# Long cross-attention of a Perceiver block: head pairs joined at their border, and a wait for GpSimd moved to where the keys are made

## The chip, the cores and the metric

The kernel runs on one core of a Trainium2 chip. The metric is the device time of one execution in microseconds. A core has TensorE (PE in the rows; PEld is its weight load), VectorE (DVE), ScalarE (ACT), GpSimd (POOL) and a queue for transfers (SP). Each engine works through its own list in order and waits for the others on semaphores.

## The reference, cut to what matters

Two layers are computed on 256 query tokens; the change touches one attention of the second layer only. With `x` of 256 x 512, a context of 4096 x 128 and 16 heads:

```python
q_hk  = (hidden_q @ Wq.T).reshape(B, S, 16, 128)
q_big = rope(einsum('bshk,hkq->bshq', q_hk, w_kc_q))      # 384 wide
kv_r  = rope(kv_c)                                        # 4096 x 128
q_r   = einsum('bshq,hqr->bhsr', q_big, W_qr)             # 64 wide
k_r   = einsum('bld,hdr->bhlr', kv_r, W_kr)
attn  = softmax(einsum('bhsr,bhlr->bhsl', q_r, k_r))      # 256 x 4096 per head
ctx_c = einsum('bhsl,bld->bhsd', attn, kv_r)
out   = einsum('bhsd,hkd->bhsk', ctx_c, w_kc_kv) @ Wo.T
```

## The kernel before, in words

Products that need more precision than one pass gives are split: a value is rounded to a high part (`keyH`, `pH`, `kvH`, `qsH`, `wkrH`, made on ScalarE) and what is left is the low part (`keyL`, `pL`, made on VectorE; `kvL`, `wkrL`, `qsL`, made on GpSimd). A product is then high by high, high by low and low by high.

**Projections.** TensorE's loop `for n in range(XH)` goes over the 16 heads: `p1(n + 1)` (8 matmuls), `p2(n)` (6 matmuls), and `p3` for a finished pair (12 matmuls). ScalarE copies the result of `p1` to `qh`, which `p2` needs and which frees bank 6 for the next `p1`. VectorE rotates the result of `p2` (`rotated(n)`: four products of PSUM with a table, the four small ones into `qm2` together with the large one into `qb`, and then the sum `qb + qm2`, L1064, both in SBUF). `p2(n + 1)` waits for the products of `rotated(n)`. Into this loop the keys of the first head pair are set at the projections that `KEYS_AT` names (`keys(0, c)`, eight stretches c of 512 keys; ScalarE makes `keyH`, VectorE `keyL`), and their scores at projections 6 to 13. The keys overwrite the rotated context in SBUF (`kvr`), from which GpSimd makes `kvL` in a single instruction; so ScalarE waits for `kvL_ready`, ahead of its first `qh`. After the loop come `keys(1, 0)`, six dummy matmuls (`stay_awake`, which only keep TensorE busy) and `p3(7)`.

**Pairs.** Then a loop over the 8 head pairs p, each over 8 stretches c of 512 keys, each over four halves e; i = 4c + e counts the 32 halves of a pair. For each half TensorE turns the exponentials (`turn(p, i)`, four transposes), ScalarE evicts them as `pH`, VectorE as `pL`, and two halves later TensorE multiplies them with the context (`weigh(p, i)`, six matmuls into bank 6, which collects the whole pair). Meanwhile the next pair is prepared: at e = 1 its keys c + 1 (`next_keys`, always through bank 7), evicted by ScalarE (`high_keys`) at e = 1 and by VectorE (`low_keys`) at e = 2; after the four halves its scores c (`scores`), which VectorE takes out in four tiles with a running maximum during the next stretch (`scores_out`, one in each half, ahead of `pL`). The four tiles of the last stretch come after the last `pL`, each followed by the small reduction that gives the row maximum (`nmX`). ScalarE makes the first stretch of exponentials from it (`first_exps`, four tiles), and the others one for each half. The finished bank 6 is copied out by `contexts_out` after the first half of the next pair, and goes through `values` and `head_out` (bank 7 too) in stretches 1 to 5. Before those, TensorE waits for the low keys in bank 7:

```python
if p and 1 <= c <= 5 and more:
    pe.wait_ge(keyL_ready, (p + 1) * NCH + c + 2)
```

At the end of a pair TensorE finishes `weigh` of its last halves before it turns anything of the next.

Of the kernel before, what the change touches and what calls it, by code (L numbers as in the profile page):

```python
# [8 lines left out]
T = 256  # L9
# [13 lines left out]
XH, XK, XQ, XR = 16, 128, 384, 64  # L23
# [3 lines left out]
NCH = L // CH  # L27
# [13 lines left out]
XP = XH // 2  # L41
SLOTS = 2 * NCH
HALVES = 4 * NCH
KEYS_AT = {1: (0,), 2: (1, 2), 3: (3, 4), 4: (5, 6), 5: (7,)}
SCORES_AT = {6 + c: c for c in range(NCH)}
TILES = ((0, 0), (1, 0), (0, 1), (1, 1))
TILES_LAST = ((0, 0), (0, 1), (1, 0), (1, 1))
# [5 lines left out]
F32 = mybir.dt.float32  # L53
# [32 lines left out]
def perceiver(nc, a, out):  # L86
    ctx = ExitStack()
    with ctx:
# [541 lines left out]
        def _(act):  # L630
# [128 lines left out]
            def high_keys(p, c, bank=7):  # L759
                act.wait_ge(key_ps, p * NCH + c + 1)  # L760
                wait(act, sX_ps, 2 * ((p - 1) * NCH + c + 1))
                act.activation(keyH[:, c * CH:(c + 1) * CH], PS[:, bank, :], ACT.Copy).then_inc(keyH_ready, 1)
# [4 lines left out]

            high_parts(0)
            high_parts(1)
            act.wait_ge(kvL_ready, 1)  # L770
            for n in range(XH):
                act.wait_ge(p1_done, n + 1)
                wait(act, p2_done, n - 1)
                act.activation(qh[:, n % 2], PS[:, 6, 0:T], ACT.Copy).then_inc(qh_ready, 1)
                for c in KEYS_AT.get(n - 1, ()):
                    high_keys(0, c, 0 if c % 2 else 7)
                if n % 2 == 0 and n >= 4:
                    ranks_out((n - 4) // 2)
                    if (n - 4) // 2 < 2:
                        high_query((n - 4) // 2)  # L780
# [7 lines left out]

            def first_exps(p):
                wait(act, csum_done, p - 1)  # L790
                for h, q in TILES_LAST:
                    exps(p, h, q, 0)

            def contexts_out(p):
# [10 lines left out]
            for p in range(XP):  # L805
                for c in range(NCH):
                    for e in range(4):
                        i = 4 * c + e
                        act.wait_ge(t_done, HALVES * p + i + 1)
                        wait(act, v_done, HALVES * p + i - 3)  # L810
                        act.activation(pH[:, i % 4], PS[:, 2 + i % 2, :].rearrange("p (k t) -> p k t", t=T), ACT.Copy).then_inc(pH_ready, 1)  # L811
                        if i == 0 and p:
                            contexts_out(p - 1)
                        if i == 8 and p:
                            values_out(p - 1)
                        if c + 1 < NCH:
                            exps(p, e // 2, e % 2, c + 1)
                        if e == 1 and c + 1 < NCH and p + 1 < XP:
                            high_keys(p + 1, c + 1)
                        if e == 1 and c + 1 == NCH and p + 2 < XP:  # L820
                            high_keys(p + 2, 0)
                        if i == 14 and p + 2 < XP:
                            high_parts(p + 2)
                            high_query(p + 2)
                if p + 1 < XP:
                    first_exps(p + 1)
# [73 lines left out]
        def _(dve):  # L900
# [165 lines left out]
            def low_keys(p, c, bank=7):  # L1066
                dve.wait_ge(keyH_ready, p * NCH + c + 1)
                at = slice(c * CH, (c + 1) * CH)
                dve.tensor_tensor(keyL[:, at], PS[:, bank, :], keyH[:, at].bitcast(F32), ALU.subtract).then_inc(keyL_ready, 1)  # L1069

            def scores_out(p, c, e):

                h, q = (TILES_LAST if c == NCH - 1 else TILES)[e]
                dve.wait_ge(sX_ps, 2 * (p * NCH + c) + q + 1)
                dve.tensor_scalar(sp_[:, h, q, c * CH:(c + 1) * CH], PS[:, 4 * q + h, :], 1.0, None, ALU.mult, ALU.max,  # L1075
                                  accum_out=cmax[:, h, q, c:c + 1]).then_inc(sX_out, 1)
                if c == NCH - 1:
                    dve.wait_ge(sX_out, 4 * (p * NCH + c) + e + 1)
                    dve.tensor_reduce(nmX[:, p % 2, h, q:q + 1], cmax[:, h, q], AX.X, ALU.max, negate=True).then_inc(nm_ready, 1)  # L1079
# [34 lines left out]
            for p in range(XP):  # L1114
                for c in range(NCH):
                    for e in range(4):
                        i = 4 * c + e
                        if c and p + 1 < XP:
                            scores_out(p + 1, c - 1, e)
                        if e == 0 and p and c in (3, 4, 5, 6):  # L1120
                            add_out(p - 1, (c - 3) // 2, (c - 3) % 2, 7)
                        dve.wait_ge(pH_ready, HALVES * p + i + 1)
                        dve.tensor_tensor(pL[:, i % 4], PS[:, 2 + i % 2, :].rearrange("p (k t) -> p k t", t=T), pH[:, i % 4].bitcast(F32),  # L1123
                                          ALU.subtract).then_inc(pL_ready, 1)
                        if e == 2 and c + 1 < NCH and p + 1 < XP:
                            low_keys(p + 1, c + 1)
                        if e == 2 and c + 1 == NCH and p + 2 < XP:
                            low_keys(p + 2, 0)
                        if c == 1 and e % 2:
                            row_max(2 * p, e // 2)  # L1130
                        if c == 6 and e % 2 and p + 1 < XP:
                            row_max(2 * p + 1, e // 2)
                if p + 1 < XP:
                    for e in range(4):
                        scores_out(p + 1, NCH - 1, e)
                dve.wait_ge(exp_done, 2 * SLOTS * (p + 1))
                dve.tensor_reduce(recX[:, p % 2], csum[:, p % 2], AX.X, ALU.add).then_inc(csum_done, 1)
                dve.wait_ge(csum_done, p + 1)
                dve.reciprocal(recX[:, p % 2], recX[:, p % 2]).then_inc(recX_ready, 1)
# [122 lines left out]
        def _(pe):  # L1262
# [208 lines left out]
            def p1(n, i, b):  # L1471

                pe.wait_ge(wqX_in[b], (i + 1) * 16)
                wait(pe, qh_ready, n)
                wait(pe, qr_ready, (n - 3) // 2)
                for kt in range(KT):
                    mm = pe.matmul(PS[:, 6, 0:T], wqX[:, b, kt, :], xnT[:, kt, :], start=(kt == 0), stop=(kt == KT - 1))
                mm.then_inc(p1_done, 1)
# [82 lines left out]
            for n in range(XH):  # L1561
                if n + 1 < XH:
                    p1(n + 1, (n + 1) // 2, (n + 1) % 2)
                p2(n, n // 2, n % 2)
                if n % 2 and n >= 3:
                    p3((n - 3) // 2)
                for c in KEYS_AT.get(n, ()):
                    wait(pe, keyL_ready, c - 1)
                    keys(0, c, 0 if c % 2 else 7)
                if n in SCORES_AT:  # L1570
                    pe.wait_ge(keyL_ready, NCH)
                    scores(0, SCORES_AT[n])
# [9 lines left out]
            for p in range(XP):  # L1582
                more = p + 1 < XP
                for c in range(NCH):
                    last = more and c + 1 == NCH
                    for e in range(4):
                        i = 4 * c + e
                        turn(p, i)
                        if i >= 2 and not (last and e == 3):
                            weigh(p, i - 2)  # L1590
                        if e == 1 and p and c:
                            pe.wait_ge(vX_ready, p - (c == 1))
                            wait(pe, oX_added, 4 * (p - 1) + min(max(c - 2, 0), 4))
                        if e == 1 and c + 1 < NCH and more:
                            next_keys(p + 1, c + 1)
                        if e == 1 and c + 1 == NCH and p + 2 < XP:
                            next_keys(p + 2, 0)
                    if p and 1 <= c <= 5 and more:
                        pe.wait_ge(keyL_ready, (p + 1) * NCH + c + 2)
                    if p and c == 1:  # L1600
                        values(p - 1)
                    if p and 2 <= c <= 5:
                        pe.wait_ge(vX_ready, p)
                        head_out(p - 1, (c - 2) // 2, c % 2, 7)
                    if more:
                        scores(p + 1, c)
                if more:
                    weigh(p, HALVES - 3)
                for i in (HALVES - 2, HALVES - 1):
                    weigh(p, i)  # L1610
            values(XP - 1)
            pe.wait_ge(vX_ready, XP)
# [217 lines left out]
```

## Time and profile before

| | |
|---|---|
| median of 3 runs | 1105.48 us (1104.18 to 1107.18) |
| the profiled execution's own time | 1111.0 us |
| its span | 1109.3 us |
| TensorE busy | 1029.9 us (93%) |
| VectorE busy | 730.3 us (66%) |
| ScalarE busy | 573.2 us (52%) |
| GpSimd busy | 268.1 us (24%) |
| projections of this attention | about 345 to 450 us of the span |
| pair 0 | about 450 to 509 us |
| pairs 1 to 6 | 66 us each, about 509 to 905 us |
| pair 7 | about 905 to 955 us |

Times in the rows are microseconds from the start of the span. In a timeline row the first number is the start, the second the duration of the (merged) instructions, and what stands in brackets is how long the engine had sat idle before them and what ended that. Matmuls overlap in the pipeline, so the start-to-start distance of two rows says more than their durations.

### The profile page before, as it was taken

The numbers are of one execution on the slowest core, as the hardware profiler recorded it, in microseconds if no ns is written. First come the engines' busy times: TensorE is split into PE (matmuls) and PEld (weight loads), VectorE is DVE, ScalarE is ACT, GpSimd is POOL, SyncE is SP. The second block draws the span as 40 slices with busy tenths as digits, with TensorE's granted clock in tenths as the row PEclk, the third lists the DMA queues.
The fourth block names the chain that finished last, engine by engine and source line by source line (L and its number), as shares of the span: only waits on it lengthen the run. The fifth ranks groups of instructions, "written<-read, shape, count | busy, mean of one in ns | idle before, by whom it ended". The sixth has DMA issues, their size and how long they took to land.

```text
span 1109.3 us, 18581 instructions
## 1 busy us (share of the span) xinstructions
PE 1029.9 (93%) x6815; PEld 813.9 (73%) x6829; DVE 730.3 (66%) x1441; ACT 573.2 (52%) x1227; POOL 268.1 (24%) x209
## 2 busy tenths in 40 slices
PE   7989999999995998999999999999999999898996
PEld 5545889999993765787777877777777779676743
DVE  3656455655533899678787777778778786463634
ACT  3345345444423210677667676675776668343423
POOL 6810144434433000022220212222021111103412
PEclk9999899999998999999999999999999999999998
DMA  9450176666502332111120111202021124403010
GB/s 275 103 230 1 23 239 210 229 232 220 200 13 90 103 89 76 47 29 32 29 55 2 53 32 30 56 1 59 27 60 40 40 64 87 165 37 157 0 62 19
DMA packets 72253, 97.49 MB, mean 88 GB/s; under 512 B 35665, under 2 KB 53233, under 8 KB 71026
## 3 DMA queue, kind: packets, MB, share of 16 engines
q1 hardware_dynamic: 72178, 96.49, 28.3%
q8 instruction: 47, 0.77, 0.3%
q14 instruction: 28, 0.23, 0.1%
HBM read 91.58 MB, written 4.90 MB: 87 GB/s over the span
## 4 chain that ended last, share of the span: by engine, by line
PE 65%; DVE 18%; ACT 9%; issue 4%; POOL 2%; DMA 1%; SPq 0%; ACTq 0%; DVEq 0%; POOLq 0%
PE PS L1418 12%; PE PS L1545 8%; PE PS L1522 7%; PE PS L1534 6%; PE PS L1437 5%; DVE pL L1123 4%; DVE scores L1075 4%; ACT pH L811 3%; PE PS L1559 3%; ACT scores L787 3%; PE PS L1507 3%; DVE keyL L1069 2%; PE PS L1266 2%; PE PS L1629 2%; PE PS L1712 1%
## 5 line engine op out<-in xcount | busy, mean ns | idle before, releaser
L1123 DVE TENSOR_TENSOR pL<-PS,pH 128x512 fp32r<-128x512 f32 x256 | 176.4, 689 | 85.9 <-ACT pH L811 84.9
L811 ACT ACTIVATE pH<-PS 128x512 fp32r<-128x512 f32 x256 | 152.6, 596 | 121.7 <-PE PS L1534 121.7
L787 ACT ACTIVATE scores<-scores,nmX 128x512 f32<-128x512 f32 x256 | 185.4, 724 | 15.8 <-DVE nmX L1079 15.8
L1075 DVE TENSOR_SCALAR_CACHE_REDUCE scores<-PS 128x512 f32<-128x512 f32 x256 | 173.0, 682 | 21.8 <-PE PS L1522 21.8
L1534 PE MATMUL PS<-ident,scores 128*128 128x128 f32 x1024 | 156.6, 277 | 10.0 <-DVE pL L1123 9.9
L1545 PE MATMUL PS<-pH,kvH 128*128 128x256 f32 x512 | 164.6, 321 | 0.0
L1534 PEld LDWEIGHTS PS<-ident,scores 128*128 128x128 f32 x1024 | 117.2, 141 | 41.9 <-DVE pL L1123 21.4
L1545 PE MATMUL PS<-pL,kvH 128*128 128x256 f32 x512 | 144.4, 282 | 0.0
L1545 PE MATMUL PS<-pH,kvL 128*128 128x256 f32 x512 | 143.9, 281 | 0.0
L1545 PEld LDWEIGHTS PS<-pH,kvH 128*128 128x128 f32 x512 | 97.2, 190 | 2.7 <-DVE pL L1123 2.7
L1545 PEld LDWEIGHTS PS<-pL,kvH 128*128 128x128 f32 x512 | 97.7, 191 | 0.0
L1545 PEld LDWEIGHTS PS<-pH,kvL 128*128 128x128 f32 x512 | 96.9, 189 | 0.0
L982 DVE TENSOR_TENSOR gL<-rawG,gH 128x1536 fp32r<-128x1536 f32 x16 | 56.9, 3557 | 29.7 <-ACT gH L671 29.5
L545 POOL TENSOR_TENSOR dL<-rawD,dH 128x1536 fp32r<-128x1536 f32 x16 | 56.4, 3525 | 49.8 <-ACT dH L715 49.8
L566 POOL TENSOR_TENSOR wkrL<-wkr,wkrH 128x128 fp32r<-128x128 f32 x8 | 3.6, 456 | 251.4 <-ACT wkrH L752 251.4
L1522 PE MATMUL PS<-keyH,qsH 64*128 64x512 f32 x256 | 59.6, 461 | 4.6 <-DVE scores L1075 4.1
L1418 PE MATMUL PS<-xH,gH 128*128 128x256 f32 x192 | 55.9, 291 | 2.4 <-DVE uL L982 2.4
L1418 PE MATMUL PS<-xH,gL 128*128 128x256 f32 x192 | 55.5, 289 | 0.0
L1418 PE MATMUL PS<-xL,gH 128*128 128x256 f32 x192 | 55.5, 289 | 0.0
L1418 PE MATMUL PS<-xH,uH 128*128 128x256 f32 x192 | 55.0, 286 | 0.0
L1418 PE MATMUL PS<-xL,uH 128*128 128x256 f32 x192 | 54.9, 286 | 0.0
L1418 PE MATMUL PS<-xH,uL 128*128 128x256 f32 x192 | 54.9, 286 | 0.0
(309 smaller groups left out, 2243.4 us busy)
## 6 DMA issues: line engine op xcount, KB each, us to landing
rawG<-in_wg SPq DMA_DIRECT2D x16, 768.0 KB, 5.6
rawU<-in_wu SPq DMA_DIRECT2D x16, 768.0 KB, 7.1
rawD<-in_wd SPq DMA_DIRECT2D x16, 768.0 KB, 6.3
xn<-in_w SPq DMA_DIRECT2D x11, 512.0 KB, 3.9
wblk<-blocks SPq DMA_DIRECT2D x4, 1056.0 KB, 9.5
wb<-w_rows SPq DMA_DIRECT2D x32, 128.0 KB, 3.3
wqX<-in_wqX SPq DMA_DIRECT2D x16, 256.0 KB, 2.6
woX<-in_woX SPq DMA_DIRECT2D x8, 512.0 KB, 4.1
```

What stands on the lines that cost most here:

```text
L545: pool.tensor_tensor(dL[:, b].rearrange("p m n -> p (m n)"), rawD[:, b], dH[:, b].rearrange("p m n -> p (m n)").bitcast(F32), ALU.subtract ...
L787: act.activation(at, at, ACT.Exp, bias=nmX[:, p % 2, h, q:q + 1], accum_out=csum[:, p % 2, NT * h + q, c:c + 1]).then_inc(exp_done, 1)
L811: act.activation(pH[:, i % 4], PS[:, 2 + i % 2, :].rearrange("p (k t) -> p k t", t=T), ACT.Copy).then_inc(pH_ready, 1)
L982: dve.tensor_tensor(lo[b][:].rearrange("p k m n -> p (k m n)"), raw[:, b], hi[b][:].rearrange("p k m n -> p (k m n)").bitcast(F32), ALU.su ...
L1075: dve.tensor_scalar(sp_[:, h, q, c * CH:(c + 1) * CH], PS[:, 4 * q + h, :], 1.0, None, ALU.mult, ALU.max, accum_out=cmax[:, h, q, c:c + 1] ...
L1123: dve.tensor_tensor(pL[:, i % 4], PS[:, 2 + i % 2, :].rearrange("p (k t) -> p k t", t=T), pH[:, i % 4].bitcast(F32), ALU.subtract).then_in ...
L1418: mm = pe.matmul(PS[:, 3 * b + m, j * T:(j + 1) * T], w[b][:, kt, m, :], v[:, kt, :], start=(kt == 0 and c == 0), stop=(kt == KT - 1 and c ...
L1437: mm = pe.matmul(PS[:, 6 + t, :], h[:, b, m, t * P:(t + 1) * P], w[:, b, m, :], start=(first and m == 0 and c == 0), stop=(last and m == 2 ...
L1507: mm = pe.matmul(PS[:, bank, :], w[:, p % 2, :], v[:, c * CH:(c + 1) * CH], start=(j == 0), stop=(j == 2))
L1522: mm = pe.matmul(PS[:, 4 * q + h, :], w[rank, p % 2, q * P:(q + 1) * P], v[rank, c * CH:(c + 1) * CH], start=(j == 0), stop=(j == 2), skip ...
L1534: mm = pe.transpose(PS[:, 2 + i % 2, m * T + q * P:m * T + (q + 1) * P], sp_[:, h, q, tile * P:(tile + 1) * P], ident[:])
L1545: mm = pe.matmul(PS[:, 6, h * T:(h + 1) * T], w[:, 4 * c + 2 * u + m, :], v[:, i % 4, m, :], start=(i == 0 and m == 0 and k == 0), stop=(c ...
```

## The change

- `KEYS_AT`: the first pair's keys are made at projections 2 to 5, two at each, where they were at 1 to 5 (1, 2, 2, 2, 1).
- ScalarE's wait for `kvL_ready` moves from before the first `qh` to before the first `keyH`.
- `low_keys` stands ahead of `pL` in its half, where it stood behind it.
- Two of the four last score tiles of the next pair are taken out before the pair's last `pL`, two behind it.
- `first_exps` makes three tiles; the fourth is made behind the next pair's first `pH`. `contexts_out` moves from behind the first `pH` to behind the second.
- TensorE's order at the border: `weigh` of halves 28 and 29 comes after the last scores, and `weigh` of halves 30 and 31 after the next pair's `turn` 0 and 1.
- Ten dummy matmuls stand ahead of `p2(14)` and ten ahead of `p2(15)`.

```diff
-KEYS_AT = {1: (0,), 2: (1, 2), 3: (3, 4), 4: (5, 6), 5: (7,)}
+KEYS_AT = {2: (0, 1), 3: (2, 3), 4: (4, 5), 5: (6, 7)}
...
             high_parts(1)
-            act.wait_ge(kvL_ready, 1)
             for n in range(XH):
...
                 for c in KEYS_AT.get(n - 1, ()):
+                    if c == 0:
+                        act.wait_ge(kvL_ready, 1)
                     high_keys(0, c, 0 if c % 2 else 7)
...
-                for h, q in TILES_LAST:
+                for h, q in TILES_LAST[0:3]:
                     exps(p, h, q, 0)
...
-                        if i == 0 and p:
+                        if i == 0:
+                            exps(p, 1, 1, 0)
+                        if i == 1 and p:
                             contexts_out(p - 1)
...
-                        dve.wait_ge(pH_ready, HALVES * p + i + 1)
-                        dve.tensor_tensor(pL[:, i % 4], PS[:, 2 + i % 2, :].rearrange("p (k t) -> p k t", t=T), pH[:, i % 4].bitcast(F32),
-                                          ALU.subtract).then_inc(pL_ready, 1)
                         if e == 2 and c + 1 < NCH and p + 1 < XP:
                             low_keys(p + 1, c + 1)
                         if e == 2 and c + 1 == NCH and p + 2 < XP:
                             low_keys(p + 2, 0)
+                        if i == HALVES - 1 and p + 1 < XP:
+                            for tile in range(2):
+                                scores_out(p + 1, NCH - 1, tile)
+                        dve.wait_ge(pH_ready, HALVES * p + i + 1)
+                        dve.tensor_tensor(pL[:, i % 4], PS[:, 2 + i % 2, :].rearrange("p (k t) -> p k t", t=T), pH[:, i % 4].bitcast(F32),
+                                          ALU.subtract).then_inc(pL_ready, 1)
...
                 if p + 1 < XP:
-                    for e in range(4):
-                        scores_out(p + 1, NCH - 1, e)
+                    for tile in range(2, 4):
+                        scores_out(p + 1, NCH - 1, tile)
...
+                if n >= XH - 2:
+                    stay_awake(10, 7)
                 p2(n, n // 2, n % 2)
...
-                        if i >= 2 and not (last and e == 3):
+                        if i >= 2 and not (last and e >= 2):
                             weigh(p, i - 2)
+                        if i < 2 and p:
+                            weigh(p - 1, HALVES - 2 + i)
...
-                if more:
-                    weigh(p, HALVES - 3)
-                for i in (HALVES - 2, HALVES - 1):
+                for i in (HALVES - 4, HALVES - 3) if more else (HALVES - 2, HALVES - 1):
                     weigh(p, i)
```

## Rows read from the trace of the kernel before

**Rows 1.** Windows: stretch, length, busy PE, PEld, DVE, ACT, POOL, granted clock, DMA, GB/s

```profile
509.00:575.00 66.00, 62.71 (x454) 51.15 (x452) 51.86 (x123) 45.49 (x108) 12.41 (x9) 1.00 0.15 36
...
443.40:449.00 5.60, 5.52 (x18) 3.09 (x18) 3.45 (x7) 0.00 (x0) 0.00 (x0) 0.50 0.00 0
...
913.00:917.00 4.00, 3.83 (x20) 3.83 (x21) 1.64 (x4) 3.24 (x10) 0.00 (x0) 0.57 0.00 0
```

**Rows 2.** Waits, 509 to 905 us: total us, times, longest

```profile
PE PS L1559 <- DVE keyL L1069: 6.9, 24, 0.5
```

**Rows 3.** Timeline at the start of the projections

```profile
345.22 1.97 PE L1477 MATMUL PS<-xnT,wqX 128*128 128x256 f32 x8 [1.78 <-issue]
...
356.49 0.38 ACT L774 ACTIVATE qh<-PS 128x256 f32<-128x256 f32 x1 [8.52 <-POOL kvL L562]
...
357.02 3.68 PE L1477 MATMUL PS<-xnT,wqX 128*128 128x256 f32 x8 [9.84 <-ACT qh L774]
...
366.31 0.96 DVE L1058 TENSOR_TENSOR qb<-PS,cosQ 128x768 f32<-128x768 f32 x1 [0.72 <-PE PS L1486]
...
371.22 1.29 ACT L762 ACTIVATE keyH<-PS 128x512 fp32r<-128x512 f32 x2 [2.10 <-PE PS L1507]
```

**Rows 4.** Timeline of VectorE and GpSimd in an earlier stage

```profile
167.78 3.81 DVE L982 TENSOR_TENSOR gL<-rawG,gH 128x1536 fp32r<-128x1536 f32 x1 [1.79 <-ACT gH L671]
171.51 1.75 DVE L982 TENSOR_TENSOR uL<-rawU,uH 128x1536 fp32r<-128x1536 f32 x1
...
166.45 3.52 POOL L545 TENSOR_TENSOR dL<-rawD,dH 128x1536 fp32r<-128x1536 f32 x1 [2.41 <-ACT dH L715]
```

**Rows 5.** Timeline inside pair 2: ends of stretches 4 and 6

```profile
615.97 0.69 DVE L1123 TENSOR_TENSOR pL<-PS,pH 128x512 fp32r<-128x512 f32 x1 [0.54 <-ACT pH L811]
616.58 0.68 DVE L1069 TENSOR_TENSOR keyL<-PS,keyH 128x512 fp32r<-128x512 f32 x1
...
616.82 0.27 PE L1545 MATMUL PS<-pH,kvL 128*128 128x256 f32 x1
617.31 1.13 PE L1559 MATMUL PS<-woX,xnT 128*128 128x512 f32 x2 [0.22 <-DVE keyL L1069]
...
633.55 0.27 PE L1545 MATMUL PS<-pH,kvL 128*128 128x256 f32 x1
633.76 0.50 PE L1522 MATMUL PS<-keyH,qsH 64*128 64x512 f32 x2
```

**Rows 6.** Timeline at the border from pair 1 to pair 2

```profile
575.03 0.68 DVE L1075 TENSOR_SCALAR_CACHE_REDUCE scores<-PS 128x512 f32<-128x512 f32 x1
...
575.78 0.50 PE L1522 MATMUL PS<-keyH,qsH 64*128 64x512 f32 x2 [0.62 <-DVE scores L1075]
...
578.77 0.72 ACT L787 ACTIVATE scores<-scores,nmX 128x512 f32<-128x512 f32 x1
...
580.77 0.59 ACT L796 ACTIVATE xnT<-PS 128x512 f32<-128x512 f32 x1
...
581.65 0.66 PE L1534 MATMUL PS<-ident,scores 128*128 128x128 f32 x4 [1.00 <-DVE pL L1123]
...
583.33 0.66 PE L1534 MATMUL PS<-ident,scores 128*128 128x128 f32 x4 [0.31 <-DVE pL L1123]
```

**Rows 7.** Timeline at the end of the projections

```profile
437.49 1.46 PE L1486 MATMUL PS<-qh,kcq 128*128 128x256 f32 x6
...
440.85 0.96 DVE L1058 TENSOR_TENSOR qb<-PS,cosQ 128x768 f32<-128x768 f32 x1
...
443.48 2.90 PE L1486 MATMUL PS<-qh,kcq 128*128 128x256 f32 x6 [4.53 <-DVE qm L1062]
446.31 2.83 PE L1498 MATMUL PS<-qb,xn 128*64 128x256 f32 x12
...
450.17 1.24 PE L1266 MATMUL PS<-busyB,identE 128*128 128x512 bf16 x5
451.35 1.52 PE L1498 MATMUL PS<-qb,xn 128*64 128x256 f32 x12
```

## The prediction

> **What bounds the kernel now.** I read the page first: TensorE is busy for 93% of the span, so only stretches in which it waits, or runs at half its clock, can give time back. The windows give a table by stage. In a pair of the middle it is busy for 62.71 of 66.00 us at full clock, VectorE for 51.86, ScalarE for 45.49 [rows 1]: TensorE sets the pace there, and the change can touch at most 3.3 us of a pair. Then the waits of pairs 1 to 6: TensorE waits 24 times, 6.9 us in all, for `keyL` ahead of `head_out` [rows 2]. Last the timeline at the edited places. It shows four of them: the start of the projections (ScalarE idle for 8.52 us and TensorE for 9.84 us, for GpSimd's `kvL`) [rows 3], their end (4.53 us idle, then half clock) [rows 1, 7], the low keys in each stretch [rows 5], and the border of two pairs [rows 6].
>
> **Wait for GpSimd moved to the keys.** ScalarE was free at 356.49 - 8.52 = 347.97; the first `p1` ended at 345.22 + 1.97 = 347.19 [rows 3]. So `qh(0)` starts at 348.0, and the second `p1` at 348.5 where it was at 357.02: 8.5 us. After 9.84 us of idleness TensorE ran that `p1` in 3.68 us; the one before it, after 1.78 us of idleness, took 1.97 [rows 3]. With only some 1.3 us idle now I take 1.97, 1.7 us more. By TensorE alone the gain is 10.2 to 10.3.
>
> VectorE takes a part of it back. Its first sum `qb + qm2` (L1064) ended 0.72 before 366.31, at 365.6, so it began at 364.6; 10.3 earlier is 354.3. But GpSimd's `kvL` runs until ScalarE is released by it, at 356.45 [rows 3]. In an earlier stage such a pair of instructions met: VectorE's 1536-element subtraction from two SBUF tensors started at 167.78 while GpSimd was in one that ended at 169.97; it took 3.81 us, its twin just after 1.75, and it ended 1.6 us after GpSimd did [rows 4]. So I count the sum as beginning when `kvL` ends: done at about 357.3. The next rotation begins then, against 366.31 before [rows 3]: from here on everything is 9.0 us early instead of 10.3.
>
> The Trainium skill, "SBUF — State Buffer", section "SBUF: two separate sides", speaks against this edit too: a VectorE instruction with two SBUF inputs and a GpSimd instruction that reads SBUF exclude each other for the whole of whichever began first. By that rule, the rows agree, the gain is 9.0; without it, 10.3.
>
> The moved wait itself should cost nothing: `keyH` of projection 2 starts at 371.22 before, about 362 now, 5.5 us after `kvL` [rows 3]. `wkrL` is queued behind `kvL` on GpSimd and wanted about a microsecond earlier than `keyH`; also there in time. The transfers of `wqX` and `kcq` move with `p1` and `p2`; the two buffers of each were loaded long before.
>
> **Keys at 2 to 5.** Projection 1 loses a set of keys, 5 gains one. The step from projection 1 to 2 is set by VectorE's rotation, so nothing is won there; in 5 the second key is ahead of `qr`, for which the next `p1` waits. Two evictions take 1.29 us [rows 3], so one more costs 0.65 to 0.7. Loss 0.7. Start in all: 9.0 - 0.7 = 8.3 (bounds 6 and 9.6).
>
> **Dummy matmuls at 14 and 15.** Five take 1.24 us [rows 7], about 0.22 each, so ten take 2.2. Those ahead of `p2(14)` push it back by 2.2 us; but its result, there at 437.49 + 1.46 = 438.95, is read by VectorE only at 440.85 [rows 7], when the scores are out. 1.9 us hide most of it; 0.35 is lost. Those ahead of `p2(15)` lie in the 4.53 us in which TensorE waits for VectorE, and keep it busy. The window behind that wait has a granted clock of 0.50, that is 1.2 GHz [rows 1]: `p2(15)` takes 2.90 us, and `p3(6)`, 12 matmuls, 2.83; the same 12 at full clock take 1.52 [rows 7]. I take 1.46 for `p2(15)`, as `p2(14)` took [rows 7]. It then starts at 443.48 + 0.35 = 443.83 and ends at 445.3, and `p3(6)` ends at 446.75 instead of 449.14: 2.4 us. `keys(1, 0)`, the six dummies and `p3(7)` follow, at 448.95 instead of 451.35 [rows 7]. ScalarE's exponentials hang on `p3(6)` and start 2.4 earlier too; one of four of them now stands behind `pH(0)`, which helps pair 0 a little. Sum 2.5 (bounds 1.5 and 3.1).
>
> **Low keys ahead of `pL`.** In stretch 4, `head_out` starts 0.49 us after the last matmul of `weigh`; where nothing is waited for, the distance is 0.21 [rows 5]. That is 0.28 lost, of which 0.22 counts as idle. Over the 24 waits the mean idle is 0.29 [rows 2], so 0.36 lost; the fifth wait of a pair, at `values`, I take at 0.26. Per pair 4 x 0.36 + 0.26 = 1.7. Can it all come back? `keyL` is issued 0.61 after `pL`, and VectorE idles 0.54 ahead of that `pL`, for `pH` [rows 5]; `keyH` is ScalarE's instruction before that `pH`. So `keyL` ends 0.6 to 1.1 us earlier, more than the longest wait of 0.5 counted (0.59 in true distance). `pL` slips by 0.1 to 0.2 us, but the first to need it is a `turn` after the scores, over 2 us later. Pairs 1 to 6: 6 x 1.7 = 10.1 (bounds 5 and 10.5; in pair 0 the wait does not exist).
>
> **The border.** Before, TensorE loses there about 0.9 us at the scores' second half (575.78), 1.2 at 581.65 and 0.5 at 583.33 [rows 6]. I lay the new order from VectorE's fourth tile of scores (575.03). It comes 0.5 earlier, since `keyL` fills an idle wait. The second half of the last scores follows 0.75 later as before. The third exponential was at 575.03 + 3.74 = 578.77 [rows 6]; the same instructions lie between in the new order, but VectorE's second tile now stands ahead of `pL` and waits some 0.37 for TensorE. So 574.53 + 3.74 + 0.37 = 578.65: 0.1 gained. From there ScalarE is busy without a pause. The copy of the contexts began 2.00 us after the third exponential [rows 6]; now one exponential (0.7) and one `pH` (0.5) more stand ahead of it, so it begins at 581.85 and ends at 582.45. `weigh(0)` of the new pair waits for it: 582.5, where it was at 582.06. `turn(3)` follows 0.8 later, 583.3, against 583.33 before. TensorE's early wait is gone and comes back as a wait for the contexts. I take 0 for each of the 7 borders (bounds 0.6 lost, by a `turn` held up behind the copy, and 1.9 gained, the idle that rows 6 count: 0.62 + 1.00 + 0.31). Into pair 7 the clock fell to a mean of 0.57 for 4 us [rows 1]; whether it does again I leave at 0.
>
> **Sum.** 8.3 + 2.5 + 10.1 + 0 = 20.9. The span would be 1088.4 and the profiled execution's own time 1111.0 - 20.9 = 1090.1. That execution stands 5.5 above the median of the runs; taken off the median, 1105.5 - 20.9 = **1084.6 us**.
>
> **The rivals.**
> - *The joined border pays.* ScalarE's start is what counts, and if the two early tiles let it run without a gap, about 1 us of the 1.9 comes back per border: 7 us more, 1077.6. For it: the order plainly separates the two engines' work. Against: the copy before `weigh(0)`. Chance 0.15.
> - *The late copy costs.* If `contexts_out` slips a further half microsecond, each border loses 0.5 to 1: about 5 us, 1089.6. For it: no slack in my layout. Chance 0.17.
> - *Head of the line at `keyL`.* VectorE now waits for `keyH` with `pL` and a tile of scores behind it. If `keyH` is late in half the stretches, 5 of the 10.1 go: 1089.7. Against: `keyH` stands ahead of `pH` on ScalarE. Chance 0.09.
> - *No change.* The gains of the start are a shift that nothing after it takes back, so this needs both other terms to turn. Chance 0.03.
> - *Slower.* The clock falls at every border: the new order has short waits at three places, and the one border with little other work already fell to 0.57 [rows 1]. A microsecond at 1.2 GHz loses half of one. The 20.9 are gone when each of 7 borders loses 3 us, that is 6 us at half clock each; with 8 us each, 1084.6 + 28 = 1112.6. Against: the windows of a pair show 1.00. Chance 0.03.
>
> **How the numbers follow.** The forecast has the rest, 0.53. A tenth of a per cent is about a microsecond here; differences under 0.3%, 3.3 us, can't be told from no change. The first four cases, 0.94, are faster by more than that; same 0.03; slower 0.03. The range 1077 to 1092 takes the two dearer rivals whole, half of the cheaper one, and the forecast with its own bounds.
>
> **What would show it.** Right: `qh(0)` near 348, the sum L1064 ending just after `kvL` with a duration of about 3 us, `keyH` with no wait for GpSimd; clock 1.00 where rows 1 show 0.50; no wait `head_out` for `keyL`; pairs of 64.4 us; at the border a wait of `weigh` for ScalarE's copy of the contexts. Wrong: pairs under 64 us (the border pays) or over 65; a granted clock under 1 at borders; a wait for the loads of `wqX` at the start.

## The result and the profile after

| | before | after |
|---|---|---|
| median (4 runs each, same chip) | 1105.39 us | 1079.51 us (1077.56 to 1080.04) |
| ratio | | 0.9761, 95% interval [0.9743, 0.9779] |
| the profiled execution: own time, span | 1111.0, 1109.3 us | 1079.65, 1077.9 us |

The change gains 25.9 us by the medians, 26.4 by the ratio (24.4 to 28.4 by the interval). The gains of the versions below are worked out from the ratio. The forecast was 1084.6 us with a range of 1077 to 1092; it was 5 us too careful. The page of the changed kernel; the columns are busy us, share of the span, instructions:

```profile
PE 1020.7 (95%) x6849; PEld 809.4 (75%) x6849; DVE 734.0 (68%) x1441; ACT 572.2 (53%) x1227; POOL 269.1 (25%) x209
```

TensorE was busy for 9.2 us more before, though the change adds 20 dummy matmuls (4.6 us): what went are, as far as the rows below show, matmuls at half its clock (`p2(15)` in 2.90 us and now in 1.53) and a longer duration right after a wait (`head_out` in 1.13 us and now in 1.02). The rest of the gain is idle time. Windows of the changed kernel, columns as in [rows 1]: a stretch of the pairs, the end of the projections, the border into pair 7, and two stretches at the first keys:

```profile
509.00:575.00 66.00, 64.22 (x475) 53.44 (x475) 54.05 (x127) 47.89 (x115) 12.47 (x8) 1.00 0.15 36
...
432.00:442.00 10.00, 9.48 (x54) 5.02 (x52) 7.31 (x15) 3.57 (x7) 0.00 (x0) 1.00 0.01 2
...
879.00:885.00 6.00, 4.59 (x37) 3.94 (x36) 3.71 (x11) 5.42 (x14) 0.00 (x0) 1.00 0.55 152
...
352.00:359.00 7.00, 3.99 (x18) 3.26 (x19) 6.79 (x9) 0.40 (x2) 3.76 (x3) 1.00 0.36 103
359.00:363.00 4.00, 4.00 (x12) 3.18 (x11) 3.21 (x7) 1.19 (x2) 0.00 (x0) 0.58 0.17 49
```

The reader sees TensorE busy for 64.22 of 66 us where it was 62.71, and 1.00 at the two places where [rows 1] has 0.50 and 0.57. But a new low clock, 0.58, stands at the first keys.

The waits of the changed kernel from 495 to 880 us (total us, times, longest). No line of TensorE names `keyL` any more, where [rows 2] had 24 waits. At the border the wait of `weigh` for the copy `xnT` is new, and the one for a tile of scores, 3.8 us in 6 waits before (509 to 905 us), has grown:

```profile
DVE keyL L1072 <- ACT keyH L762: 5.9, 6, 1.0
PE PS L1551 <- ACT xnT L797: 5.5, 6, 0.9
PE PS L1528 <- DVE scores L1078: 5.4, 7, 0.9
```

The start of the projections (timeline of the changed kernel), to be held against [rows 3]:

```profile
345.87 8.84 POOL L562 TENSOR_TENSOR kvL<-kvr,kvH 128x4096 fp32r<-128x4096 f32 x1 [7.90 <-ACT kvH L747]
...
346.61 1.97 PE L1483 MATMUL PS<-xnT,wqX 128*128 128x256 f32 x8 [1.21 <-ACT qh L773]
...
352.51 3.02 DVE L1067 TENSOR_TENSOR qb<-qb,qm 128x768 f32<-128x768 f32 x1
...
358.27 1.54 PE L1492 MATMUL PS<-qh,kcq 128*128 128x256 f32 x6 [2.39 <-DVE qm L1065]
...
360.04 0.63 PE L1513 MATMUL PS<-kvTL,wkrH 128*128 128x512 f32 x1
```

The second `p1` starts while `kvL` has just begun, and takes 1.97 us. The sum `qb + qm2` meets `kvL` and lasts 3.02 us. TensorE then waits 2.39 us at `p2(2)`, its clock falls, and a key matmul takes 0.63 us where it takes 0.39 at full clock. The end of the projections:

```profile
432.54 2.32 PE L1272 MATMUL PS<-busyB,identE 128*128 128x512 bf16 x10
435.38 1.53 PE L1492 MATMUL PS<-qh,kcq 128*128 128x256 f32 x6 [0.52 <-DVE qm L1065]
436.84 1.52 PE L1504 MATMUL PS<-qb,xn 128*64 128x256 f32 x12
...
440.10 0.72 ACT L788 ACTIVATE scores<-scores,nmX 128x512 f32<-128x512 f32 x1
```

`p2(15)` and `p3(6)` take 1.53 and 1.52 us where [rows 7] have 2.90 and 2.83. The end of stretch 4 in pair 2, which answers to [rows 5]:

```profile
600.56 0.28 PE L1551 MATMUL PS<-pH,kvL 128*128 128x256 f32 x1
600.67 1.02 PE L1565 MATMUL PS<-woX,xnT 128*128 128x512 f32 x2
```

The distance from the last `weigh` matmul to `head_out` is 0.11 us, where it was 0.49 with the wait, and the two matmuls of `head_out` take 1.02 instead of 1.13. And the border from pair 1 to 2, which answers to [rows 6]:

```profile
558.93 0.69 DVE L1072 TENSOR_TENSOR keyL<-PS,keyH 128x512 fp32r<-128x512 f32 x1
...
560.13 0.68 DVE L1078 TENSOR_SCALAR_CACHE_REDUCE scores<-PS 128x512 f32<-128x512 f32 x1
...
560.88 0.50 PE L1528 MATMUL PS<-keyH,qsH 64*128 64x512 f32 x2 [0.85 <-DVE scores L1078]
...
567.30 0.58 ACT L797 ACTIVATE xnT<-PS 128x512 f32<-128x512 f32 x1
...
568.03 0.36 PE L1551 MATMUL PS<-pH,kvH 128*128 128x256 f32 x1 [0.91 <-ACT xnT L797]
```

The wait for `pL` became one for the copy of the contexts (0.91), and the wait for a tile of scores grew from 0.62 to 0.85.

**Where the time went.** The gain of the profiled execution is 1109.3 - 1077.9 = 31.4 us. Of it 1.78 lie ahead of the edited code (`kvH` starts at 343.97 before, at 342.19 after) and 1.77 behind pair 7: the two executions differ there by chance, and these two explain most of why the spans differ by more than the medians. The clock shows it: both kernels run the same instructions there, and the mean granted clock is 0.72 from 118 to 130 us and from 965 to 977 before, against 0.86 from 117 to 129 and from 936 to 948 after. The rest I read from `kvH` to the first exponential, and then between the first matmuls of `scores` of each stretch, which every version has in the same order:

| part | before | after | gained |
|---|---|---|---|
| `kvH` to the first exponential (450.89 and 440.10) | 106.92 | 97.91 | 9.0 |
| from there to the first `scores` of pair 1 (518.55 and 506.85) | 67.66 | 66.75 | 0.9 |
| from there to the first `scores` of pair 6 (849.09 and 823.25), five pairs | 330.54 | 316.40 | 14.1 |
| the rest of pair 6 and pair 7, what is left of 31.4 - 3.55 | | | 3.8 |

The 9.0 are 6.6 at the start (read at `p2(6)`: 391.86 before and 383.44 after, less the 1.78) and 2.4 at the end of the projections. Of the 3.8, 2.9 lie before the last `scores` of pair 6 (904.50 and 875.79) and 0.9 behind them. In pair 1 the stretches, from one `scores` to the next, took 8.37, 8.65, 8.36, 8.37, 8.34, 7.04 and then 16.94 us for the last one with the border; now they take 7.90, 7.88, 7.89, 7.88, 7.88, 7.03 and 16.75. A pair went from 66.07 to 63.21 us.

### The profile page after: what moved, and what is told of

Same layout as the page of the kernel before. It is cut to its first block, busy times and chain, and to the rows that moved or that the text cites. A ratio compares the mean times of both kernels' runs of the same rounds, so it can differ in the third digit from the quotient of the medians.

```text
span 1077.9 us, 18635 instructions
## 1 busy us (share of the span) xinstructions
PE 1020.7 (95%) x6849; PEld 809.4 (75%) x6849; DVE 734.0 (68%) x1441; ACT 572.2 (53%) x1227; POOL 269.1 (25%) x209
## 4 chain that ended last, share of the span: by engine, by line
PE 79%; DVE 12%; ACT 5%; issue 2%; DMA 1%; POOL 1%; SPq 0%; DVEq 0%; ACTq 0%; POOLq 0%
PE PS L1551 16%; PE PS L1424 12%; PE PS L1540 10%; PE PS L1528 8%; PE PS L1443 5%; PE PS L1513 4%; DVE scores L1078 2%; PE PS L1565 2%; PE PS L1272 2%; PE PS L1637 2%; ACT scores L788 1%; PE PS L1720 1%; PE PS L1646 1%; PE PS L1324 1%; PE PS L1483 1%
## 5 line engine op out<-in xcount | busy, mean ns | idle before, releaser
L1528 PEld LDWEIGHTS PS<-keyH,qsH 64*128 64x128 f32 x256 | 24.0, 183 | 42.3 <-issue 24.5
```

Of the source, the lines that this page charges most:

```text
L1528: mm = pe.matmul(PS[:, 4 * q + h, :], w[rank, p % 2, q * P:(q + 1) * P], v[rank, c * CH:(c + 1) * CH], start=(j == 0), stop=(j == 2), skip ...
```

## The experiments

The first question was where the gain of the pairs comes from. Theory A: low keys ahead of `pL` are worth nearly 3 us per pair, and the joined border nothing. Theory B, by my own sizes: a removed wait is worth what I forecast (1.7 us per pair), and the joined border brings the rest. A kernel's time stands beside runs of the kernel before on the same chip.

**Low keys alone.** The kernel before with

```diff
+                        if e == 2 and c + 1 < NCH and p + 1 < XP:
+                            low_keys(p + 1, c + 1)
...
                         dve.wait_ge(pH_ready, HALVES * p + i + 1)
                         dve.tensor_tensor(pL[:, i % 4], ...
-                        if e == 2 and c + 1 < NCH and p + 1 < XP:
-                            low_keys(p + 1, c + 1)
```

> The kernel before with one part alone: low_keys ahead of pL. Theory A (the term was mis-sized): a wait of TensorE ahead of head_out costs 0.48 us and not 0.28, because the load of its weights is no longer hidden behind the last weigh, and pair 0 gains 0.2 us a stretch too, because VectorE's fourth tile of scores is out sooner. Then stretches 1 to 5 of pairs 1 to 6 give 2.7 us a pair and pair 0 about 1: 17 us, about 1088.5. Theory B (the term was right, the border gave the rest): 10 us, about 1095.5, and stretches 3 to 5 shorter by 0.28 each.

1088.23 us against 1107.38, ratio 0.9827 [0.9799, 0.9855]: 19.2 us. From the first `scores` of pair 1 to that of pair 2 are 62.84 us (515.44 to 578.28), 3.2 less than before, and below the 63.21 of the changed kernel; two later pairs of this execution were 0.9 and 0.6 us longer than such pairs are in the versions below. From the first exponential to the last `scores` of pair 6 this one edit gains 18.6 us, more than the whole change there (17.9). B falls. In pair 0, where there is no wait for `keyL`, the stretches fall from 7.20 to 7.03 us too: VectorE's tile of scores comes earlier, and TensorE's second half of `scores` follows the first after 0.80 us instead of 0.87, with its two matmuls at 0.39 instead of 0.50.

**The start alone** (`KEYS_AT` and the moved wait):

```diff
+KEYS_AT = {2: (0, 1), 3: (2, 3), 4: (4, 5), 5: (6, 7)}
...
-            act.wait_ge(kvL_ready, 1)
...
+                    if c == 0:
+                        act.wait_ge(kvL_ready, 1)
```

> The kernel before with the start alone: the wait for GpSimd at the first key, and the first pair's keys at projections 2 to 5. By the prediction's term 8.3 us, 1097. In the changed kernel's trace TensorE fell to half clock at the keys of projection 2, which took 1.6 us of it; Theory A: that happens here too, 6.5 us, 1099. Theory B (the low clock there was chance): 8.3 us.

1099.47 us, ratio 0.9935 [0.9912, 0.9959]: 7.2 us. From `kvH` to the first exponential are 100.36 us, 6.56 less than before. The low clock at the first keys is there too (and in two versions below with the same start, the one without the border part and the one with the copy of the contexts back: 0.67 and 0.66 from 356 to 361 us). Its windows:

```profile
352.00:359.00 7.00, 4.60 (x20) 3.65 (x18) 5.68 (x7) 0.38 (x1) 2.49 (x3) 0.90 0.30 87
359.00:363.00 4.00, 4.00 (x15) 3.25 (x15) 3.52 (x7) 1.20 (x2) 0.00 (x0) 0.76 0.18 49
```

**The dummies alone** (`stay_awake(10, 7)` ahead of `p2(14)` and `p2(15)`):

> The kernel before with the twenty dummy matmuls ahead of p2(14) and p2(15) alone. By the prediction's term 2.4 us at the first exponentials, 1103; granted clock 1.00 where it was 0.50. The rival: the dummies only keep TensorE from work that was ready, and the exponentials start no sooner, 1105.4.

1105.0 us, ratio 0.9986 [0.9964, 1.0009]: the median can't tell it from nothing, but the trace can. From `kvH` (342.96) to the first exponential (447.49) are 104.53 us, 2.39 less than before, with the clock at 1.00.

**The joined border alone** (the other three edits undone):

```diff
+                for h, q in TILES_LAST[0:3]:
...
+                        if i == 0:
+                            exps(p, 1, 1, 0)
+                        if i == 1 and p:
                             contexts_out(p - 1)
...
+                        if i < 2 and p:
+                            weigh(p - 1, HALVES - 2 + i)
```

> The kernel before with the border alone: three first exponentials, the contexts' copy behind the second pH, two score tiles ahead of the last pL, weigh of halves 30 and 31 behind the next pair's turns; low_keys stays behind pL. By the prediction's layout 0 per border. Here VectorE's fourth tile is not 0.5 us earlier, so the third exponential and all behind it come 0.4 later: 0 to 3 us slower in all, 1105 to 1108. Theory B (the border gave what the prediction lacked): 1 us less per border, 1098.

1108.18 us, ratio 1.001 [0.9989, 1.003]. A pair takes 66.40 us (515.86 to 582.26), 0.33 more than before. TensorE's waits from 510 to 910 us, which holds six borders (total us, times, longest):

```profile
PE PS L1527 <- DVE scores L1077: 6.8, 6, 1.3
PE PS L1550 <- ACT xnT L796: 5.5, 6, 0.9
```

They are 1.13 and 0.92 us per border, together more than the 0.62 + 1.00 + 0.31 of [rows 6]. From the second half of the last scores (573.09) to the third exponential (576.43) it takes 3.34 us, where [rows 6] have 2.99.

**The changed kernel without the border part.**

> The changed kernel without its border part (start, low_keys and dummies stay): four first exponentials, the contexts' copy behind the first pH, all four score tiles behind the last pL, weigh in the old order. If the border is worth nothing in its place (the prediction's layout: 0.1 us at each of 7), the time is that of the changed kernel, 1079.5 to 1080.5. If it gave what the prediction lacked, about 5 us more, 1085. The trace of the changed kernel shows TensorE idle for 0.85 and 0.91 us at a border; here waits of about 0.4, 1.0 and 0.3 as before.

1076.65 us against 1105.08, ratio 0.9732 [0.9697, 0.9767]: not slower, and in the trace 0.37 us per pair faster (62.84, from 504.75 to 567.59). Its border from pair 1 to 2:

```profile
558.01 0.68 DVE L1076 TENSOR_SCALAR_CACHE_REDUCE scores<-PS 128x512 f32<-128x512 f32 x1
...
558.75 0.50 PE L1523 MATMUL PS<-keyH,qsH 64*128 64x512 f32 x2
...
564.62 0.66 PE L1535 MATMUL PS<-ident,scores 128*128 128x128 f32 x4 [1.01 <-DVE pL L1128]
...
566.29 0.66 PE L1535 MATMUL PS<-ident,scores 128*128 128x128 f32 x4 [0.31 <-DVE pL L1128]
```

Its third exponential, and that of the changed kernel:

```profile
561.74 0.72 ACT L788 ACTIVATE scores<-scores,nmX 128x512 f32<-128x512 f32 x1
...
564.21 0.72 ACT L788 ACTIVATE scores<-scores,nmX 128x512 f32<-128x512 f32 x1 [0.58 <-DVE nmX L1082]
```

The 0.62 that [rows 6] show ahead of the second half of the scores is gone without the border part: `keyL` now fills an idle wait of VectorE, so its tile of scores is out in time. The joined order brings a wait back at that place, since it takes the `weigh` of one half (28; that of 29 stood behind the scores already) away from ahead of the scores, which had covered VectorE's tile. But this wait by itself costs nothing: counted from the first matmul of the scores before (551.17 here, 553.31 in the changed kernel), the second half of the last scores starts 7.58 us later here and 7.57 there, and the `weigh` that went is only done later. What does come later is ScalarE's work, since VectorE's second tile, now ahead of `pL`, waits for TensorE: the third exponential follows the second half of the scores after 2.99 us here (558.75 to 561.74), as before (575.78 to 578.77), and after 3.33 in the changed kernel (560.88 to 564.21). Idle per border: 1.32 us here, 0.85 + 0.91 = 1.76 in the changed kernel; the difference of 0.44 stands beside 0.37 of the period.

**The copy of the contexts back behind the first `pH`** (`if i == 0 and p: contexts_out(p - 1)`, after the fourth exponential):

> The changed kernel with contexts_out back behind the first pH (but behind the fourth exponential, which stands there now). The prediction says that the late copy gives back what the joined border wins, because weigh(0) waits for it. The copy then ends about 1.2 us earlier and weigh(0) with it, but turn(3) next waits for pL(1), which the copy now delays by 0: so 0.2 us at each border, 1.4 in all, 1078. If the copy is the only thing in the way, 0.9 at each border, 6 us, 1073.5. If the copy waits for weigh of half 31 on TensorE and holds ScalarE up with it: slower, 1082.

1077.26 us, ratio 0.9743 [0.9711, 0.9774]. A pair takes 63.09 us (504.34 to 567.43), 0.12 less than in the changed kernel. The late copy carries a third of the border's loss. The rest, 0.25, goes with the later third exponential: it still stands 3.34 us behind the second half of the scores (558.34 to 561.68), where it is 2.99 without the border part. The wait for a tile of scores, 5.4 us over 7 borders in either kernel's wait table, is the same in both and doesn't delay what stands behind it.

**`kvL` in four instructions of GpSimd.** The question is whether VectorE's sum is shut out for as long as one GpSimd instruction lasts, or is slowed by the traffic of both engines.

```diff
-            pool.tensor_tensor(kvL[:], kvr[:], kvH[:].bitcast(F32), ALU.subtract).then_inc(kvL_ready, 1)
+            for part in range(4):
+                rows = slice(8 * part, 8 * part + 8)
+                ins = pool.tensor_tensor(kvL[:, rows], kvr[:, rows], kvH[:, rows].bitcast(F32), ALU.subtract)
+            ins.then_inc(kvL_ready, 1)
```

> The changed kernel with GpSimd's kvL in four instructions of 1024 elements a partition instead of one of 4096. If VectorE's sum of two SBUF tensors is shut out for the whole of a GpSimd instruction, it now ends within 2.2 us of when it is ready instead of at the end of kvL: its duration falls from 3.0 us to at most 2.2, or below 1.9 where it comes right behind a boundary, and all that follows is 0.8 to 1.3 us earlier, if TensorE's clock does not eat it. If the two instructions merely share bandwidth, the duration stays near 3 us.

1076.33 us, ratio 0.973 [0.9699, 0.9761]. Its timeline (the four instructions merged, then the first and the fourth alone) and windows:

```profile
346.35 10.00 POOL L564 TENSOR_TENSOR kvL<-kvr,kvH 128x1024 fp32r<-128x1024 f32 x4 [8.93 <-ACT kvH L750]
...
346.35 2.35 POOL L564 TENSOR_TENSOR kvL<-kvr,kvH 128x1024 fp32r<-128x1024 f32 x1 [8.93 <-ACT kvH L750]
...
352.99 1.14 DVE L1070 TENSOR_TENSOR qb<-qb,qm 128x768 f32<-128x768 f32 x1
...
353.28 3.08 POOL L564 TENSOR_TENSOR kvL<-kvr,kvH 128x1024 fp32r<-128x1024 f32 x1
...
357.31 1.53 PE L1495 MATMUL PS<-qh,kcq 128*128 128x256 f32 x6 [0.95 <-DVE qm L1068]
```

```profile
352.00:359.00 7.00, 5.03 (x23) 4.11 (x23) 5.61 (x11) 0.77 (x2) 4.85 (x4) 1.00 0.40 118
359.00:363.00 4.00, 4.00 (x20) 3.32 (x18) 3.94 (x8) 1.58 (x3) 0.00 (x0) 1.00 0.24 52
```

The sum takes 1.14 us instead of 3.02 in the midst of GpSimd's work, so it is the length of one GpSimd instruction that counts. The exclusion shows on both sides: the first three instructions take 2.35 us each, and the third ends at 353.32; the sum ends 0.8 us after that, as it ended 0.8 us after the single long `kvL` (355.53 and 354.71); and the fourth, which meets the sum, takes 3.08, 0.73 more than the others. The sum came only 0.33 us before the third ended. Right behind the start of one it would have stood there for up to 2.35 (an estimate from these rows), so 1.14 is close to the best case of this split. TensorE's wait falls from 2.39 to 0.95, and the clock stays at 1.00. From `kvH` to the first exponential are 94.91 us, 3.0 less than in the changed kernel. In the medians the gain isn't resolved.

**Dummies ahead of `p2(1)` and `p2(2)`** (4 and 10 in the changed kernel):

> The changed kernel with four dummy matmuls ahead of p2(1) and ten ahead of p2(2), where TensorE is idle for 1.02 and 2.39 us and then runs the keys of projection 2 at a granted clock of 0.58. Theory: the idleness brought the clock down, and the dummies keep it up: the keys and the next p1 take 1.6 us less, time 1078. Rival: the clock falls there all the same, or the dummies push p2 back by what they win: no change.

1078.72 us, ratio 0.9759 [0.9724, 0.9794], that is no change in the median. `kvL` is one instruction here and the sum takes 3.04 us, but the clock stays at full speed. Its windows:

```profile
352.00:359.00 7.00, 6.75 (x32) 4.63 (x31) 6.10 (x11) 1.49 (x3) 1.03 (x2) 1.00 0.31 93
359.00:363.00 4.00, 4.00 (x25) 2.76 (x24) 3.95 (x8) 0.48 (x2) 0.00 (x0) 1.00 0.27 86
```

From `kvH` (339.44) to the first exponential (435.80) are 96.36 us, 1.55 less than in the changed kernel. So of the 3.0 that the split brings, about 1.55 is the clock and about as much the shorter sum (`p2(2)` starts 1.44 earlier there, counted from `kvH`).

**The two findings together**: the changed kernel without its border part and with the split `kvL`.

> The changed kernel without its border part and with kvL made in four instructions. Theory A (the pieces are independent): against the changed kernel the border part costs 0.4 us in each of six pairs (a pair took 62.84 us without it and 63.23 with it), so 2.4 us, and the single long kvL costs 3 us at the projections (table load less start of kvH 96.62 before the split, 93.61 with it). Some 1074 us where the kernel before stands at 1105. Theory B: neither shows in the medians, 1077 to 1079 us.

1075.0 us against 1107.59, ratio 0.9708 [0.9678, 0.9739], the fastest of all; a pair takes 62.86 us, and `kvH` to the first exponential takes 94.89. Against the changed kernel (0.9761) it is 0.5% better; the two intervals just miss each other, but the two kernels were not run side by side.

**The same with the keys where they were** (`KEYS_AT` of before):

> As the version without the border part and with kvL in four instructions, but with the keys where they were, at projections 1 to 5; the wait for kvL stands ahead of the first keyH. Theory A: the first keyH now asks for kvL some 4 us earlier, at about 353 us, while kvL ends at 356.4, so ScalarE waits 3 us with the copy to qh behind it, and about 2 of these reach TensorE; against that projection 5 has one key less, 0.7. So 1 to 2 us slower than its neighbour in this call, with an idle TensorE and perhaps a low clock at projection 2. Theory B (the second key ahead of qr at projection 5 is what costs): 0.7 us faster.

1076.81 us, ratio 0.9712 [0.9683, 0.9742]. In the trace `kvH` to the first exponential takes 96.33 us, 1.44 more. The place wasn't the one I had named. Its timeline:

```profile
355.41 0.45 POOL L569 TENSOR_TENSOR wkrL<-wkr,wkrH 128x128 fp32r<-128x128 f32 x1
...
355.92 0.50 PE L1511 MATMUL PS<-kvTH,wkrH 128*128 128x512 f32 x1 [2.34 <-POOL wkrL L569]
```

TensorE waits 2.34 us for `wkrL`, which is queued behind `kvL` on GpSimd; ScalarE's wait for `kvL` is over by then. With the moved wait, making the keys at projection 2 pays for itself in the trace by covering this; the medians (1076.81 and 1075.0) don't resolve it. Its windows, over the same stretches as above:

```profile
352.00:359.00 7.00, 4.62 (x20) 3.75 (x21) 5.20 (x8) 0.95 (x2) 3.78 (x4) 1.00 0.22 66
359.00:363.00 4.00, 4.00 (x20) 3.43 (x19) 3.00 (x6) 1.22 (x3) 0.00 (x0) 1.00 0.45 115
```

So 2.34 us of idleness, after one of 1.03 a little earlier, were not followed by a low clock here, where 2.39 after 1.02 were in the changed kernel. The length of the wait alone doesn't tell it.

**Low keys ahead of `pL` in stretches 1 and 2 alone**, in the kernel before:

```diff
+                        if c in (1, 2) and e == 2 and c + 1 < NCH and p + 1 < XP:
+                            low_keys(p + 1, c + 1)
```

> The kernel before, with low_keys ahead of pL only in stretches 1 and 2 of a pair. Theory A (each removed wait is worth its idle plus a start of TensorE that is hidden again, and the waits are independent): the two stretches that then have no wait give 0.5 to 0.8 us each, a pair takes 66.06 - 1.2 = 64.9 us, and the time falls by about 7 to 8 us, to 0.993. Theory B (the 2.84 us of a pair come from the whole order of VectorE, which only runs ahead when all waits are gone): under 0.36 a wait as I had sized them, a pair of 65.3 us or more, 4 us in all.

1100.05 us, ratio 0.9939 [0.9912, 0.9965], 6.8 us. A pair takes 64.84 us (517.27 to 582.11). Its first two stretches take 7.88 us each, 0.49 and 0.77 less than before; the third still takes 8.35. The wait table has 18 waits left:

```profile
PE PS L1561 <- DVE keyL L1069: 3.8, 18, 0.2
```

The gain is local to the stretch in which the wait goes, and more than the 0.26 and 0.36 of the prediction. The six waits for `head_out` that are gone held 6.9 - 3.8 = 3.1 us, 0.52 each, where their stretch gives 0.77; those that are left hold 0.21 each, and their stretches give 0.47 to 0.49 in the changed kernel. Either way a removed wait is worth its idle time and about 0.26 more.

## Why the prediction was right, and which term was too small

**Wait for GpSimd moved: right up to `p2(2)`.** That instruction starts at 368.95 before and 358.27 after, 10.68 earlier, 8.90 without the 1.78 that lie ahead; the forecast had 9.0. It rested on the exclusion of the two engines, which gives back 1.3 of 10.3. The Trainium skill, "SBUF — State Buffer", section "SBUF: two separate sides", has it as a lock held for one instruction. The traces agree: 3.02 us for the sum with one long `kvL`, 1.14 with four short ones, and the fourth of these longer by 0.73 itself.

**Start in all: 8.3 forecast, 6.6 measured.** The 0.7 for the second key in projection 5 is there: from `p2(5)` to `p2(6)` it takes 7.34 us where it took 6.66. What was missing is the clock: I looked only at whether `p1` would be slow after its wait, and saw that the 9.84 us of idleness were gone. That failed: the 2.39 us that were left at `p2(2)` were still followed by a granted clock of 0.58, and by a low one in all four kernels that have this start, one long `kvL` and no dummies there; by `p2(3)`, after the two keys, 8.90 had become 7.31 (373.44 before, 364.35 after). The version with dummies there keeps the clock at 1.00 and gets 1.55 back.

**End of the projections: 2.5 forecast, 2.4 in the ledger, 2.39 alone.** Right term by term.

**Low keys: 10.1 forecast (6 x 1.7 is 10.2), 17.0 in the table above for pairs 1 to 6 together with the border part, 19.2 alone.** This is the term that was mis-sized. First, I took 0.21 us, the distance to `scores` in [rows 5], as what is left when `head_out` doesn't wait. It is 0.11, and `head_out` itself takes 0.11 less, so that place gives 0.49 and not 0.28. The rows show where the 0.11 of `head_out` come from: with the wait its weight load starts together with its first matmul (617.31 both), without it 0.11 ahead (600.56 and 600.67). The stretches of pair 1 gained 0.47, 0.77, 0.47, 0.49 and 0.46, together 2.66 and not 1.7. Second, the low keys in stretch 7 make the border faster by 0.53 (16.94 before, 16.41 without the border part): the wait of 0.62 for a tile of scores goes. I had seen that the tile comes 0.5 earlier, but booked it inside the border's layout, where the other edits ate it. Third, pair 0 gains 0.8 in stretches that have no such wait; I had written that nothing is to be had there. The bound of 10.5 was too low, since it held a wait's worth to be its idle time and one start.

**The border: 0 forecast.** The layout was right in what sets the border's length: the copy of the contexts at its new place is what `weigh(0)` waits for, 0.91 us, VectorE's second tile does wait for TensorE (the 0.37 of the layout; the third exponential is 0.34 later than without the border part), and with the 0.5 that the tile comes earlier the third exponential hardly moves. It was wrong in that TensorE's wait for a tile of scores doesn't go, it grows from 0.62 to 0.85. Taken alone the border part costs 0.33 us per pair; with the 0.53 that the low keys give at the same place it comes out at +0.2. The rival *the joined border pays*, which would have given about the time measured (1077.6 against 1079.5), is refuted as a cause: without the border part the kernel isn't slower. That the time lies within the range is in part luck: the range held because one mis-sized term, outside its own bounds, lay within the room that this refuted rival had made, and because the start fell short by 1.7 on the other side.

**Head of the line at `keyL`, and slower by the clock: no.** VectorE waits for `keyH` at one place of a pair only, 1.0 us just after the border, and TensorE doesn't wait for that `keyL`. The windows read at borders show a clock of 1.00, the one into pair 7, 0.57 before, among them, which the sum had left at 0.

That the low clock at the border into pair 7 is gone can't be put down to the change. The start alone and the dummies alone have the code of the pairs as it was; the first has the low clock there and the second doesn't. Their windows at that border:

```profile
903.00:907.00 4.00, 3.68 (x20) 3.48 (x19) 2.03 (x3) 3.13 (x9) 0.00 (x0) 0.58 0.03 4
...
909.70:913.70 4.00, 3.81 (x31) 3.59 (x32) 2.18 (x4) 4.00 (x11) 0.00 (x0) 1.00 0.00 0
```

From the last `scores` of pair 6 to the last `weigh` of pair 7 it takes 50.13 us before and 50.11 in the first, 48.84 in the second: the low clock is worth 1.3 us there and differs between executions of the same code. With it the ledger closes: 31.4 - 1.78 - 1.77 - 1.3 = 26.6 us for the change, beside 26.4 by the ratio.

What stays open: what decides whether the clock falls after a wait. The versions with 2.39 and with 2.34 us of idleness differ in it, and so do two executions with the same code of the pairs.

## What to carry to other kernels

When TensorE paces a stretch and waits briefly for one tile, look at what the engine that makes the tile did just before: if it idled for another operand, swapping the two instructions can be free, as it was here, and the gain was larger than the idle shown by about 0.26 us a wait, since the next instruction's start is covered again. Measure the natural distance to the same instruction, not to another one. A wait that grows in the table need not cost anything; look at whether the instruction behind it starts later, and follow the chain that does (here the third exponential). And where a long GpSimd instruction overlaps VectorE's work on two SBUF tensors, cut it in pieces: VectorE then waited for the rest of one piece, and not for the whole.

## What the hardware showed that was not expected

- An idle time of 2.39 us of TensorE was followed by a mean granted clock of 0.58 from 359 to 363 us, with matmuls of 0.63 us in place of 0.39; with 0.95 us of idleness in its place, or with dummies, it was 1.00. In another version it was 1.00 after an idle time of 2.34.
- VectorE's sum of two SBUF tensors took 3.02 us beside one GpSimd instruction of 8.84, ending 0.8 us after it, 1.14 beside four that took 10.00 together, and 0.96 by itself. The split costs GpSimd 1.16 us, of which 0.73 is its fourth instruction's meeting with the sum, and saves VectorE 1.9.
